# Routed experts' closing slot: gate sums, w2 products, FFN rows and the last slot's normalisation in another order

## What is computed

```python
h = _L0_tok_ref(x, L0_tok_W, L0_tok_b)
h = h + _L0_attn_ref(_layernorm(h), ...)
h = h + _L0_ffn_ref(_layernorm(h), ...)      # shared FFN + routed experts
h = h + _L1_attn_ref(_layernorm(h), ...)     # causal, polymax
h = h + _L1_ffn_ref(_layernorm(h), ...)      # ternary weights
# in _L0_ffn_ref
    routed_in = xf[flat_idx] * weights
    h = silu(_grouped_mm(routed_in, w1, counts)) * _grouped_mm(routed_in, w3, counts)
    routed_out = _grouped_mm(h, w2, counts)
    out = shared.at[flat_idx].add(routed_out)
# in _L1_attn_ref: att = polymax(masked scores); y = att @ v; return y @ W_proj
# in _L1_ffn_ref: h = gelu(x / rms @ sign(w_up).T); return h / rms @ sign(w_down).T
```

## Time and profile before

| | us |
|---|---|
| median of three runs | 810.17 (809.11 to 811.44) |
| profiled execution, its own time | 813.9 |
| its span in the trace | 811.8 |
| PE busy in it | 691.7 |
| DVE busy in it | 616.6 |
| ACT busy in it | 425.7 |
| mean granted clock of PE | 0.928 of full |

### The profile page before, as it was taken

One profiled execution on the slowest core, in us unless ns is written; L12 is line 12 of the kernel. 1 busy time (PEld: TensorE's weight loads), 2 busy tenths in 40 slices (PEclk: granted clock), 3 DMA queues, 4 the chain that ended last, 5 costly groups with the idle time before them and its releaser, 6 DMA issues.

```text
span 811.8 us, 26981 instructions
## 1 busy us (share of the span) xinstructions
PE 691.7 (85%) x11581; PEld 492.2 (61%) x11581; DVE 616.6 (76%) x1393; ACT 425.7 (52%) x653; POOL 89.3 (11%) x76
## 2 busy tenths in 40 slices
PE   5878999999999999965783789899999998888766
PEld 4565676767685858654372557565767665565634
DVE  6676878888888888688477777878979896656643
ACT  4535455554546373543324484956667682745413
POOL 0101212020202020100000101001010100000000
PEclk9889999999999999986875999999999999999959
DMA  9025202020201000200000000000000000000000
GB/s 313 34 77 185 80 0 78 0 78 0 78 0 58 19 0 2 105 2 1 0 2 2 1 3 27 3 28 2 26 0 0 26 3 27 2 27 2 29 1 27
DMA packets 8547, 27.40 MB, mean 34 GB/s; under 512 B 3617, under 2 KB 4385, under 8 KB 6945
## 3 DMA queue, kind: packets, MB, share of 16 engines
q1 hardware_dynamic: 8480, 26.42, 9.1%
HBM read 22.22 MB, written 4.19 MB: 33 GB/s over the span
## 4 chain that ended last, share of the span: by engine, by line
PE 50%; DVE 19%; ACT 16%; issue 11%; SPq 2%; DMA 1%; POOL 1%; DVEq 0%; ACTq 0%; POOLq 0%
PE PS L378 7%; PE PS L327 6%; PE PS L389 5%; PE PS L488 4%; PE PS L717 3%; PE PS L368 3%; PE PS L763 3%; PE PS L477 3%; PE PS L432 3%; DVE mx L1351 3%; DVE Pm L1357 3%; ACT w_s L1056 3%; PE PS L751 2%; PE PS L443 2%; PE PS L707 2%
## 5 line engine op out<-in xcount | busy, mean ns | idle before, releaser
L920 ACT ACTIVATE PT<-PS 128x512 f32<-128x512 f32 x64 | 36.7, 596 | 70.2 <-PE PS L477 70.2
L730 PE MATMUL PS<-xT,wqkv_h 128*128 128x512 f16 x256 | 64.1, 398 | 9.1 <-DVE xT L1729 4.6
L368 PE MATMUL PS<-ident_s,xn 128*128 128x128 f32 x256 | 43.7, 303 | 25.7 <-DVE xn L1272 12.6
L327 PE MATMUL PS<-tokW_h,w_s 128*128 128x256 f16 x504 | 58.5, 273 | 0.0
L913 ACT ACTIVATE Pm<-Pm 128x1024 f32<-128x1024 f32 x32 | 33.1, 1054 | 46.7 <-DVE Pm L1357 46.7
L730 PEld LDWEIGHTS PS<-xT,wqkv_h 128*128 128x128 f16 x256 | 23.4, 101 | 47.7 <-ACT w_s L1056 16.2
L368 PEld LDWEIGHTS PS<-ident_s,xn 128*128 128x128 f32 x256 | 31.1, 150 | 34.8 <-ACT vbuf L1023 11.1
L327 PEld LDWEIGHTS PS<-tokW_h,w_s 128*128 128x128 f16 x504 | 48.6, 98 | 5.8
L443 PE MATMUL PS<-kM,qT 32*64 32x128 f32 x2048 | 51.6, 292 | 0.0
L1260 DVE BATCH_NORM_STATS2 st<-H 128x6 f32 (+1 forms) x128 | 46.3, 413 | 2.5
L477 PE MATMUL PS<-ident_s,Pm 128*128 128x128 f32 x256 | 41.1, 297 | 7.3 <-DVE Pm L1357 7.0
(11 more groups left out here) (250 smaller groups left out, 1587.7 us busy)
## 6 DMA issues: line engine op xcount, KB each, us to landing
work<-in_x SPq DMA_DIRECT2D x7, 1536.0 KB, 6.4
out<-H SPq DMA_DIRECT2D x8, 512.0 KB, 2.6
w_s<-in_w SPq DMA_DIRECT2D x3, 1024.0 KB, 6.9
work<-in_x SPq DMA_DIRECT2D x3, 512.0 KB, 5.5
wup_s<-in_wup SPq DMA_DIRECT2D x1, 1024.0 KB, 6.2
wdn_s<-in_wdn SPq DMA_DIRECT2D x1, 1024.0 KB, 6.9
w_s<-in_tokW SPq DMA_DIRECT2D x3, 256.0 KB, 4.1
wup_s<-in_wqkv SPq DMA_DIRECT2D x1, 768.0 KB, 7.7
```

The costliest lines, as they stand in the source:

```text
L327: m = pe.matmul(dst, halves_[xi][:, k, rows], w[:, wi, k, cols], start=(n == 0), stop=(n == 3 * chunks - 1))
L368: m = pe.transpose(PS[:, bank, t * P:(t + 1) * P], xn[:, t, c * P:(c + 1) * P], ident_s[:, :])
L730: m = pe.matmul(PS[:, UP_BANKS[f % 3], :], wup_h[:, c, f * P:(f + 1) * P], part[:, c, :], start=(k == 0), stop=(k == 2 * C - 1))
```

## The change

In slot 5 alone, on PE: the fold product becomes a function of its own, `gate_turn`, and is issued behind the value products of tiles 2 and 3 and V's tile 0, ahead of the projection; the w2 products (`routed_out`) follow V's tiles 1 to 3 instead of the projection. On DVE: `gated_sums` stands ahead of `norm4` of tiles 0 and 1 instead of behind `stats4` of tiles 2 and 3; `v_x4T` stands ahead of slot 7's `stats3` and `minus_mean3`. On ACT: slot 7's `a_norm3` moves out of slot 5 into slot 6, behind the copy of yT for tiles 0 and 1 and ahead of the copies of the transposed xn1. The condition `nxt and not ahead` holds for slot 6 only. Nothing is added or taken away: every engine has as many instructions as before. Below line 638 the new file's lines are three further on in PE's functions and six further on in the other engines'.

```diff
--- before.py
+++ after.py
@@ -636,10 +636,13 @@
                     if k == RB // 2 - 1 or k == RB - 1:
                         m.then_inc(z_mm, 1)
 
-            def routed_out():
+            def gate_turn():
 
                 pe.wait_ge(racc_ok, LAST - 2)
                 pe.matmul(PS[:, 0, 0:64], racc[:, :], fold[:, :], start=True, stop=True).then_inc(gT_mm, 1)
+
+            def routed_out():
+
                 pe.wait_ge(gT_ok, 1)
                 for e in range(NX):
                     m = pe.matmul(PS[0:NX, 1, 0:E], gT[:, e * NX:(e + 1) * NX], w2_s[:, e, :],
@@ -818,13 +821,16 @@
                 B2_values(g, 1)
                 if nxt:
                     B1_v(g + 1, (0,))
+                if routed == "last":
+                    gate_turn()
                 B2_proj(g, 1, 4)
                 if routed in ("first", "batch"):
                     routed_gates(g)
-                elif routed:
+                if nxt:
+                    B1_v(g + 1, range(1, TILES))
+                if routed == "last":
                     routed_out()
                 if nxt:
-                    B1_v(g + 1, range(1, TILES))
                     pe.wait_ge(Bv_out, 2 * g + 3)
                 else:
                     pe.wait_ge(h5_ok, TILES * g)
@@ -1069,6 +1075,8 @@
                 if not prev:
                     a_norm3(g + 1)
                 a_turned(g, 0)
+                if nxt and not ahead:
+                    a_norm3(g + 1)
                 if nxt:
                     a_B1_x(g + 1)
                 if routed in ("first", "batch"):
@@ -1083,8 +1091,6 @@
                     a_B1_v(g + 1, 0)
                 if routed in ("first", "batch"):
                     routed_tanh(g, 0)
-                if routed == "last":
-                    a_norm3(g + 2)
                 a_B3_x(g)
                 if nxt:
                     a_B1_v(g + 1, 1)
@@ -1786,6 +1792,8 @@
                 stats4(g, 0)
                 if routed in ("batch", "last"):
                     sums_in(g)
+                if routed == "last":
+                    gated_sums()
                 norm4(g, 0)
                 if ahead and routed != "last":
                     stats3(g + 2)
@@ -1793,8 +1801,6 @@
                 stats4(g, 1)
                 if ahead and routed != "last":
                     minus_mean3(g + 2)
-                if routed == "last":
-                    gated_sums()
                 if routed in ("first", "batch"):
                     gates_in(g, (0,))
                 norm4(g, 1)
@@ -1802,10 +1808,10 @@
                     gates_in(g, (1,))
                 elif routed:
                     routed_rows_in()
+                v_x4T(g)
                 if routed == "last":
                     stats3(g + 2)
                     minus_mean3(g + 2)
-                v_x4T(g)
                 if nxt:
                     v_quads(g + 1, 0)
                     v_quads(g + 1, 1)
```

## The result

| | before | after |
|---|---|---|
| median of eleven runs each, side by side | 812.11 us | 805.44 us |
| ratio of after to before | | 0.993, 95% interval 0.9906 to 0.9953 |
| the same comparison made again | 811.32 us | 804.92 us, ratio 0.9922 (0.9894 to 0.995) |
| profiled execution, its span | 811.8 us | 802.5 us |

The forecast was 803.4 us, 6.8 off the median. The two medians are 6.7 apart. The ratio, which goes by all runs, says 5.7 us off 812 (3.8 to 7.6), the second comparison 6.3. The direction held, and the size lies within the interval. Several of the steps behind them did not hold, and the profiled pair itself differs by 9.3 us, not by 6.8.

What follows compares the result with a forecast made beforehand. PE was taken as the bound, waiting in slot 5 through the order of DVE and ACT work. Terms 4.0 + 3.0 + 0.3 - 0.5 = 6.8 us off the 810.17 us median gave 803.4 us, range 800.7 to 806.3.

Steps and rivals of the forecast that it cites:

- part 4: Slot 6 on ACT: four normalisations of 2.07 us moved there, ending 1.5 us before PE wants xn, priced at nothing.
- so the pause comes along: Slot 6's Gram products: PE's 2.37 us pause, read as waiting for code, stays at the same products, only earlier.
- slots 6 and 7 and the tail shift as a block: Behind slot 5: everything later moves earlier alike, by the summed 6.8 us.
- part 1: Slot 5: gate sums turned earlier, w2 products later at full clock; transposes start 4.0 us earlier.
- part 3: Slot 6: slot 7's statistics on DVE delay squares by 1.8 us; cost 0.5 us, bounds 0 and 1.9.
- The chain (parts 1 and 2): Slot 5: w2 through normalisations to up; gate-sum reordering gives 4.0 us, FFN rows ahead of statistics and normalisations 3.0.
- DVE's new wait: Slot 5: `gated_sums` waits for PE's fold product; fits by 0.2 us, taken as 0, bounds 0 to 0.8.
- The 0.3 us behind the up products: Slot 5, first up product to next value products: without the gap it takes slot 6's 10.08 us, not 10.38.
- rival B: Slot 6: PE's pause goes, its transposes end 9.2 us earlier, 801.0 us; chance 0.11.

Runs made afterwards that it cites:

- part 1 alone: The changed kernel without its edits on ACT and to `v_x4T`; ratio to the kernel before 1.0005 (0.9979 to 1.0032).
- parts 2 to 4 alone: The kernel before with only the ACT and `v_x4T` edits; ratio to the kernel before 0.9968 (0.994 to 0.9997).
- second profile of before: The kernel before, run and profiled again with no edit; ratio 1.0008 (0.9981 to 1.0035).
- the first pair: The first profile of the kernel before and of the changed kernel; spans 811.8 and 802.5 us.
- third profile of after: The changed kernel with no edit, profiled a third time; it ends 125.6 us behind the start of slot 5's second value products.
- normalised twice: The changed kernel with slot 7's four normalisations done twice on ACT in slot 6; ratio to the kernel before 0.9925 (0.9897 to 0.9953).
- late statistics: The changed kernel with slot 7's statistics and nm moved behind DVE's low parts of slot 5's gelus; ratio to the kernel before 0.9933 (0.9907 to 0.9959).

## Why the prediction was right or wrong

The step that failed is part 4's "so the pause comes along", with what the sum drew from it, that slots 6 and 7 and the tail shift as a block. The pause kept its place and not its length, 0.69 us in place of 2.37, and slots 6 and 7 became shorter themselves. Two terms of the sum were also mis-sized: part 1's 4.0 us, 2.5 at the upper clock, and part 3's 0.5, about 0.2.

**The chain (parts 1 and 2): right.** It is w2, rows, statistics, POOL, normalisations, x4, up: with part 1 alone PE idles 5.00 us for it. The up products came at 12.5 to 12.6 behind the value products where I had 12.5 (691.2 - 678.66), the w2 products in 3.55 to 3.62 us where I had 3.45, and DVE's new wait cost nothing, with 0.1 us to spare (its normalisations end at 684.06, its add starts at 684.17).

**The term of part 1: over-sized by what it was counted from.** Of its 4.0 us, 1.7 were the lower clock in the w2 products. The wait of 2.15 us is the kernel's own; that the clock fell behind it is not. It fell in two profiles of before out of three, and not in the run with parts 2 to 4 alone. Against the second profile of before, which lacks it, the transposes come 2.5 us earlier, the up products 5.5, slot 6's values 5.5 (the sum had 4.0, 7.0 and 7.3). The 0.3 us behind the up products was the lower clock as well: that stretch is 10.38 us in two profiles of before and 10.05 in the one that has none, and 10.06 in all three of after. The sum mixed what always happens with what happened in the one execution. The forecast took all of it off a median of three runs, 810.17, which eleven put at 812.11. (680.86 + 7.51 is 688.37, not 688.35; nothing hangs on it.)

**Part 3: the price of 0.5 was too high.** The squares came 1.6 us late where I had 1.8, and PE stopped at the second half of the values (0.36 us). But DVE also stopped PE twice in the Gram products, and borders of the code lie behind these stops: the pauses there grew by nearly as much when the stops went. Taking the delay away gave 0.2 us at slot 6's down products, and nothing that the timed runs can tell.

**Part 4: wrong step.** "The pause comes along" held for its place, to the product, and not for its length: it ends when the next block is there, 3.45 to 4.01 us behind the entry into the block before. What DVE's stops delay behind that entry comes out of the pause. In the first pair 2.37 became 0.69: the 125th Gram product ends 1.1 us later behind the entry, and the block came 0.55 us sooner (3.45 against 4.00), which differs from one execution to the next: the third profile of after has 4.00 again, and a pause of 1.38. The lower clock behind the pause fell in two of three profiles of before (2.37 and 2.38 us of pause) and in one of three of after (1.38); it also fell behind 1.11 us (normalised twice) and not behind 1.83 (part 1 alone). That the shorter pause took it away is not shown. What did go is the cover of the normalisations: their 1.5 us to spare became about -0.4, which costs about 0.2 us (transposes 1.25 us long, not 1.04). In the first pair slot 6's transposes come 9.2 us earlier, the figure of rival B, to which I gave 0.11. That is luck: the other two pairs give 7.1 and 6.2, and rival B had a pause that does not return.

**The tail as one block: wrong.** Before the transposes of slot 6's FFN rows are through, PE waits the same 2.41 us in every profile of both kernels. From the first of them to the up products it takes 6.6 to 6.9 us in all three of before and in the third of after, and 5.5 in two of the three of after, by the lower clock or its absence. On the mean of three profiles each, slot 6's values come 6.7 us earlier, its transposes 7.5, slot 7's values 8.6 and the end 8.7 (132.6 to 123.9), 2 more than the 6.8.

**Luck in the sum.** The forecast's errors offset one another. At slot 6's values it had 7.3 us, where 5.5 come without the lower clock. For part 3 it took off 0.5, where about 0.2 was due. For slots 6 and 7 it had nothing, where the profiles show 2.0 more on their means. That 6.8 lies near the timed 5.7 to 6.3 is in part luck.

**What stays open.** The three profiles of before end at 132 to 133 and take 810.6 to 817.0 us, mean 813.8, those of after 804.6 to 807.6, mean 806.4: 7.4 us. That is 1.3 less than the 8.7 counted from slot 5's value products, because the executions differ ahead of them too, where the kernels are the same: they start at 676 to 683 us in the three of before and at 679.8 to 681.7 in those of after. The timed difference is 5.7 to 6.3, with an interval of about 2 to each side. The profiles exceed the timed gain in the variants too, by 3.1 us with part 1 alone, 4.1 with parts 2 to 4 alone, 1.2 with the late statistics and 0.2 normalised twice. So at least part of the excess lies with the three executions of before that were profiled, mean 813.8 us against medians of 811.3 to 812.6. No run here settles the rest, nor how much of what the profiles show in slots 6 and 7 the timed runs have.

## What to carry to other kernels

A wait of one execution is a property of the kernel when a second profile repeats it to the hundredth; the clock behind the wait is not, so price a removed gap at the upper level, and the clock's share as a bound. Two edits on one chain must be summed at the chain's end: PE's 2.5 us at the transposes were worth 0.5 at the up products and nothing in the time, because the rows' statistics still stood between. Where an engine pauses with no releaser, ask where its code blocks end, and expect such a pause to swallow what is saved between the entry into a block and its end.

## What the hardware showed that I had not expected

The loop of slots 2 to 4 has 832 matmuls and 878 weight loads per pass, and its second and third passes show no pause for code and no packet of the instruction queue. A hundred instructions far ahead of it, on an idle PE, made each later pass 8 to 9 us longer (from one slot's first up product to the next's 51.8 and 53.1 us in place of 43.8) and the kernel 17 to 19 us slower; 24 and 256 did not. The Trainium skill, page "Runtime: NRT & Kernel Launch", section "Instruction fetch mechanics", gives blocks of 256 instructions and 2048 instructions of room for PE. The runs agree on the blocks, to the product. They also fit a body of some 1,700 instructions that stays in that room at one place of its borders and not at another, though no run here measured the room itself. The same section of the Trainium skill says that the fetch is hidden by the issue rate. At these small products it is not: 125 Gram products with their loads, 250 instructions, pass in 1.2 us (703.91 to 705.11 in the run with the late statistics), and PE then stood for 2.37.
